# Two attentions over 257 keys on one Trainium2 core: scores in two halves, the last key in one product, heads summed on VectorE

## The reference, cut to what matters

```python
# x: (128, 32, 128), ctx: (128, 257, 128); 16 heads of 8 features
q = heads(x @ Wq.T); k = heads(ctx @ Wk.T); v = heads(ctx @ Wv.T)   # layer 1: q, k normalised per head
s = einsum('bhqd,bhkd->bhqk', q, k)                # layer 2: masked keys get -inf
p = softmax(s)                                     # over 257 keys
out = einsum('bhqk,bhkd->bhqd', p, v)
x = x + (join_heads(out) @ Wo.T + bo)
```

## Time and profile before

| | before |
|---|---|
| median of 3 runs | 4020.48 us (4013.39 to 4028.0) |
| profiled execution, first to last instruction | 4018.7 us |
| l1x_att, first to last scores | 827.0 to 1330.5 us |
| l2x_att, first to last scores | 1905.4 to 2469.8 us |
| PE, DVE, ACT, POOL busy in the whole | 78%, 60%, 51%, 49% |

### The profile page before, as it was taken

One profiled execution on the slowest core, in us unless ns is written; L12 is line 12 of the kernel. 1 busy time (PEld: TensorE's weight loads), 2 busy tenths in 40 slices (PEclk: granted clock), 3 DMA queues, 4 the chain that ended last, 5 costly groups with the idle time before them and its releaser, 6 DMA issues. The chain is left out here.

```text
span 4018.7 us, 81101 instructions
## 1 busy us (share of the span) xinstructions
PE 3136.4 (78%) x24323; PEld 2160.5 (54%) x24323; DVE 2425.2 (60%) x5893; ACT 2065.1 (51%) x6409; POOL 1963.5 (49%) x1960
## 2 busy tenths in 40 slices
PE   6969587779999597675999997788773458867966
PEld 4759434456666486553777775233332235744645
DVE  7956586656666474243666665698894312456862
ACT  5545306657777454323666665454541114557954
POOL 4630205656666695053555554788880251116830
PEclk9979698989999798787999998899896676987978
DMA  3300002312222000111111110443332125910000
GB/s 96 91 19 0 6 3 72 98 59 68 66 66 68 21 2 6 53 39 47 31 29 30 30 29 27 142 138 137 137 121 86 20 49 152 230 25 5 2 7 21
DMA packets 138613, 233.70 MB, mean 58 GB/s; under 512 B 28428, under 2 KB 100398, under 8 KB 137623
## 3 DMA queue, kind: packets, MB, share of 16 engines
q1 hardware_dynamic: 130264, 221.60, 18.8%
q0 software_dynamic: 8128, 9.45, 1.3%
HBM read 200.43 MB, written 13.71 MB: 53 GB/s over the span
## 5 line engine op out<-in xcount | busy, mean ns | idle before, releaser
L2427 POOL TENSOR_TENSOR l2x_att_prob<-l2x_att_prob,l2x_att_rs 128x1024 f32<-128x1024 f32 x128 | 242.2, 1893 | 253.2 <-DVE l2x_att_rs L2671 253.2
L3200 PE MATMUL l2a_pY<-l2a_hc,ident 128*128 128x512 f32 x512 | 275.0, 677 | 90.3 <-POOL l2a_hc L3119 56.1
L2427 POOL TENSOR_TENSOR l1x_att_prob<-l1x_att_prob,l1x_att_rs 128x1024 f32<-128x1024 f32 x128 | 242.2, 1893 | 190.6 <-DVE l1x_att_rs L2671 190.6
L2626 ACT ACTIVATE l2x_att_prob<-l2x_att_pS,l2x_att_nmx 128x257 f32<-128x257 f32 x512 | 236.2, 474 | 169.4 <-DVE l2x_att_nmx L2666 169.4
L3089 POOL TENSOR_TENSOR l2a_dbu<-l2a_dx,l2a_BC 128x1024 f32<-128x1024 f32 x128 | 298.5, 2352 | 21.5 <-PE l2a_pY L3200 10.7
L2626 ACT ACTIVATE l1x_att_prob<-l1x_att_pS,l1x_att_nmx 128x257 f32<-128x257 f32 x512 | 236.2, 474 | 129.7 <-DVE l1x_att_nmx L2666 129.7
L3217 ACT ACTIVATE l2a_pA<-l2a_dl,l2a_A 128x512 f32<-128x512 f32 x256 | 174.4, 689 | 188.8 <-DVE l2a_pH L3323 113.0
L3200 PEld LDWEIGHTS l2a_pY<-l2a_hc,ident 128*128 128x128 f32 x512 | 103.7, 211 | 253.2 <-issue 120.0
L3323 DVE TENSOR_TENSOR_SCAN l2a_pH<-l2a_pA,l2a_dbu 128x512 f32<-128x512 f32 x192 | 224.8, 1216 | 23.6 <-POOL l2a_dbu L3089 12.2
L2666 DVE TENSOR_REDUCE l2x_att_nmx<-l2x_att_pS 128x2 f32<-128x514 f32 x256 | 165.5, 688 | 115.7 <-PE l2x_att_pS L2534 113.0
L2666 DVE TENSOR_REDUCE l1x_att_nmx<-l1x_att_pS 128x2 f32<-128x514 f32 x256 | 165.5, 689 | 92.4 <-PE l1x_att_pS L2527 92.3
(11 more groups left out here) (735 smaller groups left out, 9284.2 us busy)
## 6 DMA issues: line engine op xcount, KB each, us to landing
l2a_BC<-l2a_rows SPq DMA_DIRECT2D x128, 512.0 KB, 3.8
l3x_att_ctn<-ctx_n SPq DMA_DIRECT2D x32, 576.0 KB, 13.9
l0x_att_kvs<-ctx_t SPq DMA_DIRECT2D x32, 514.0 KB, 3.5
l1x_k_xin<-ctx_t SPq DMA_DIRECT2D x32, 514.0 KB, 3.5
l1x_att_ctx<-ctx_t SPq DMA_DIRECT2D x128, 128.5 KB, 2.1
l1x_att_kT<-l1x_KA SPq DMA_DIRECT2D x128, 128.5 KB, 2.2
l2x_att_ctx<-ctx_t SPq DMA_DIRECT2D x128, 128.5 KB, 2.1
l3x_att_ctx<-ctx_t SPq DMA_DIRECT2D x32, 514.0 KB, 11.6
```

Of the source, the lines that this page charges most:

```text
L2427: pool.tensor_tensor(p, p, bc(rs[:, b, :], 2, LAST), ALU.mult).then_inc(scaled, 1)
L2626: last = act.activation(prob[:, b, j, 0:KEYS], pS[:, j, 0:KEYS], ACT.Exp, bias=nmx[:, b, j:j + 1], accum_out=sums[:, b, j:j + 1])
L3200: last = pe.matmul(pY[c][:, :], env.ident[:, :], hc[:, u % 3, c, :], start=False, stop=n == NS - 1)
```

## The change

- `scores` takes a half, u, and is called twice in a slot: groups 0 and 1 at the slot's start, groups 2 and 3 behind `attend`. Each waits only for its own half of p_made and announces itself once. In l2x_att the mask products are split in the same way.
- DVE takes maxima(n+1, 0), then factors(n), own_head(n-2), then maxima(n+1, 1).
- The last key: vm, tail, pbd and mt are laid out on all 128 partitions (32 for each group, half of it zeros, cleared once). `last_keys` is one product of 128 x 128, `turn_tails` four small products of 32 x 32, `pbd` 128 x 128, and its share of `output` one product. They now stand in slots 0 (last_keys) and 1 (turn_tails, pbd).
- DVE sums own over the four groups (`sum_heads`, a reduction of 128 x 512 to 128 x 128, tile osum) in slot 1, and `output` is one product osum x wo and one pbd x mt.
- On POOL the bias of x is added behind `queries`, and two memsets stand ahead of the loop.

```diff
@@ on TensorE
-                def scores(n, c, k):
+                def turn_tails():
+                    for h in range(R):
+                        r = slice(32 * h, 32 * h + 32)
+                        last = pe.matmul(PT[r, :], tail[r, :], env.ident[r, r])
+                    last.then_inc(pt_made, 1)
+
+                def last_keys(k):
+                    pe.wait_ge(vm_made, made(k))
+                    after(pe, mo_kept, k - 1)
+                    pe.matmul(M, vm[:, :, :].rearrange("p h j -> p (h j)"), wo[:, :]).then_inc(mo_made, 1)
+
+                def scores(n, c, k, u):
                     b = (c + 1) % 2
-                    pe.wait_ge(q_made, made(n))
...
-                    after(pe, p_made, 2 * (n - 1) + 1)
-                    for j in range(R):
+                    after(pe, p_made, 2 * (n - 1) + u)
+                    for j in (2 * u, 2 * u + 1):
                         r = slice(32 * j, 32 * j + 32)
...
+                    last.then_inc(s_made, 1)
...
                 def output(g):
-                    pe.wait_ge(own_made, made(4 * g + 3))
-                    for h in range(R):
-                        pe.matmul(X, own[:, h].rearrange("p b q -> p (b q)"), wo[:, :], start=h == 0, stop=False)
-                    pe.wait_ge(mo_kept, made(2 * g + 1))
+                    pe.wait_ge(osum_made, made(g))
+                    pe.matmul(X, osum[:, :, :].rearrange("p b q -> p (b q)"), wo[:, :], start=True, stop=False)
+                    pe.wait_ge(mo_kept, made(g))
                     pe.wait_ge(pb_made, made(g))
-                    for h in range(R):
-                        last = pe.matmul(X, pbd[:, h].rearrange("p b q -> p (b q)"), mt[:, h, :], start=False,
-                                         stop=h == R - 1)
-                    last.then_inc(out_made, 1)
+                    pe.matmul(X, pbd[:, :, :].rearrange("p b q -> p (b q)"), mt[:, :], start=False, stop=True
+                              ).then_inc(out_made, 1)
 
                 def slot(n, c, k):
                     if inside(n + 1):
-                        scores(n + 1, c, k)
+                        scores(n + 1, c, k, 0)
+                    if c == 1 and inside(n - 5):
+                        pe.wait_ge(tail_kept, made(2 * (k - 1) + 1))
                     if inside(n - 2):
                         attend(n - 2, (c - 2) % 4, k if c >= 2 else k - 1)
+                    if c == 1 and inside(n - 5):
+                        turn_tails()
+                    if inside(n + 1):
+                        scores(n + 1, c, k, 1)
                     if inside(n + 2) and KA is None:
                         keys(n + 2, c, k)
...
@@ on VectorE
+                def sum_heads(k):
+                    dve.wait_ge(own_made, made(4 * k + 3))
+                    after(dve, out_made, k - 1)
+                    dve.tensor_reduce(osum[:, :, :].rearrange("p b q -> p (b q)"),
+                                      own[:, :, :, :].rearrange("p h b q -> p (b q) h"), AX.X, ALU.add
+                                      ).then_inc(osum_made, 1)
...
                 def slot(n, c, k):
-                    if inside(n):
-                        factors(n, c)
                     if c == 2 and inside(n - 6):
                         add(k - 1)
                     if inside(n + 1):
                         maxima(n + 1, (c + 1) % 4, 0)
-                        maxima(n + 1, (c + 1) % 4, 1)
+                    if inside(n):
+                        factors(n, c)
                     if inside(n - 2):
                         own_head(n - 2, (c - 2) % 4, k if c >= 2 else k - 1)
-                    if c == 0 and inside(n - 4):
-                        dve.wait_ge(pt_made, made(k - 1))
+                    if c == 1 and inside(n - 5):
+                        keep_tails(k - 1)
+                    if inside(n + 1):
+                        maxima(n + 1, (c + 1) % 4, 1)
+                    if c == 1 and inside(n - 5):
+                        sum_heads(k - 1)
                     if inside(n + 2) and KA is None:
                         keys(n + 2, c)
-                    if c == 0 and inside(n - 4):
-                        keep_tails(k - 1)
                     if inside(n - 1):
                         keep_turned(n - 1, (c - 1) % 4)
```

More of the change, by code:

```diff
@@ L2370, in cross_attention @@
         cl, vt = st.sb("cl", [P, B]), st.sb("vt", [P, B])
-        m16, batch16 = st.sb("m16", [P, R, R]), st.sb("batch16", [16, BT])
-        vm, tail = st.sb("vm", [P, R, 16]), st.sb("tail", [P, BT, R])
-        pbd, mt = st.sb("pbd", [16, R, BT, S]), st.sb("mt", [16, R, D])
+        m16, batch32 = st.sb("m16", [P, R, R]), st.sb("batch32", [P, BT])
+        vm, tail = st.sb("vm", [P, R, 32]), st.sb("tail", [P, 32])
+        pbd, mt = st.sb("pbd", [P, BT, S]), st.sb("mt", [P, D])
+        osum = st.sb("osum", [P, BT, S])
         nmx, sums, rs = (st.sb(n, [P, 4, R]) for n in ("nmx", "sums", "rs"))
@@ L2415, in _ @@
                 st.open(pool)
+                pool.memset(vm[:, :, :], 0.0).then_inc(cleared, 1)
+                pool.memset(tail[:, :], 0.0).then_inc(cleared, 1)
                 pool.wait_ge(loaded, 16 * len(loads))
                 pool.wait_ge(vt_kept, 1)
+                pool.wait_ge(cleared, 2)
                 def queries(n, b):
@@ L2451, in slot @@
                         queries(n + 2, c + 2)
+                    if c == 0 and inside(n):
+                        x = env.X[:, k, :]
+                        pool.tensor_tensor(x, x, bo[:, :], ALU.add).then_inc(biased, 1)
                     if c == 1 and inside(n):
@@ L2528, in scores @@
                                          start=True, stop=not masked)
-                        if not masked and j % 2:
-                            last.then_inc(s_made, 1)
                     if masked:
-                        for j in range(R):
+                        for j in (2 * u, 2 * u + 1):
                             r = slice(32 * j, 32 * j + 32)
@@ L2642, in slot @@
                         values(n + 2, c)
-                    if c == 3 and inside(n):
-                        last_keys(k, 0)
                     if c == 0 and inside(n - 4):
-                        last_keys(k - 1, 1)
+                        last_keys(k - 1)
                 run_slots4(act, slot, B, -2, 3)
@@ L2691, in own_head @@
                     dve.wait_ge(o_made, made(n))
-                    after(dve, out_made, k - 1)
+                    if b == 3:
+                        dve.wait_ge(pt_made, made(k))
+                    if b == 0:
+                        after(dve, osum_made, k - 1)
                     o, m = O.rearrange("p (h q) -> p h q", q=S), bc(env.m4[:, :], 2, S)
```

70 lines of the change are left out of this document (27 added, 43 removed).

## The result

The changed kernel takes 4074.97 us (median of 4 runs, 4064.68 to 4082.06); the kernel before, beside it, 4020.24 us (4013.39 to 4028.0). The ratio is 1.0131, with a 95% interval of 1.0108 to 1.0154: 1.3% slower. Forecast were 4041.5 us. The direction is right and the time is inside the range, but of a loss of 21 us that was forecast, 55 came.

A forecast was written before the change was run, and what follows sets the result against it. TensorE was taken as busiest, with a ring over ACT's copy binding l1x_att and TensorE's work l2x_att, plus a kT wait in slot 1. +6 and +15 us made +21 on 4020.48: 4041.5 us, range 3997 to 4078.

The forecast's parts named there:

- A half costs as much as the whole: Scores on TensorE: each half another 0.65 us a slot in l1x_att, 0.76 in l2x_att; +2.6 and +3.0 us a round.
- The ring over ACT: l1x_att slots 2, 3, 0: attend, second-half scores, maxima, exponentials, ACT's probT copy, next attend; 3.88 us against TensorE's 3.4.
- The last key: TensorE: output from 16 passes to 4, 1.32 us less a round; turn_tails 0.2; the 0.80 wait for pbd goes.
- The first (PE alone): Rival: TensorE alone sets both stages, the new ring does not bind, kT in time; 3997 us, chance 0.12.
- The second and third (a half costs less): Rivals on scores: two groups cost half of four, 3918 us, chance 0.05; a half is 0.55, 4000 us, chance 0.05.
- The fourth: Rival on TensorE: new changes of shape cost 0.1 more at each half, together +39; 4080 us, chance 0.12.
- the forecast of +6: l1x_att: round 16.01 against 15.83, +0.18, times 32 rounds.

The follow-up runs named there:

- the two kernels that open the ring at different places: Changed kernel with factors ahead of the first maxima on DVE, 4031.91 us; changed kernel with queries ahead of scale on POOL, 4033.77 us.
- the kernel with factors first: Changed kernel with factors(n) ahead of maxima(n+1, 0) on DVE, as before the change: 4031.91 us, ratio 1.0004.
- With both opened: Changed kernel with queries ahead of scale on POOL and ACT's copy of probT between the two halves of the exponentials: 3983.97 us, ratio 0.9917.
- the best version: Changed kernel with score halves side by side, queries ahead of scale and keys ahead of sum_heads: 3873.37 us, ratio 0.9658.
- the sum behind the keys: Changed kernel with whole scores, factors ahead of the maxima and sum_heads behind the keys on DVE: 3943.31 us, ratio 0.9777.
- copy between: Changed kernel with factors ahead of the maxima and ACT's copy of probT between the two halves of the exponentials: 4032.81 us, ratio 1.0008.
- no sum: Changed kernel with whole scores, factors ahead of the maxima, and four output products in place of sum_heads: 3938.10 us, ratio 0.9787.
- halves adjacent: Changed kernel with both score halves side by side ahead of attend, a wait each, and queries ahead of scale: 3910.86 us, ratio 0.9698.
- queries first: Changed kernel with queries(n+2) ahead of scale(n) and tails on POOL: 4033.77 us, ratio 1.0012.

## Why the prediction was right and wrong

**The step that failed** is the sentence "POOL and ACT are far from full, and the memsets lie beside the loads: nothing for them." It prices POOL by how busy it is. The sum did work out a new ring, but only for ACT; it moved factors behind the first maxima, as the order on VectorE shows, and never asked who waits for factors. POOL's scale does, the queries stand behind scale, and PE's next scores wait for the queries. Every link was in the code. In the trace of before, scores and their weight loads waited for ACT's prob (44.0 us in the whole of l1x_att) and not for qb, because scale needed only exponentials that were already under way. The cost is 1.14 us a round in l1x_att and 0.50 in l2x_att, 50 to 52 us in both stages, shown by the two kernels that open the ring at different places.

**The rest of the sum was too dear, by 16 to 19 us.** With the ring open the stages stand 2.3 and 4.5 us above before, where the forecast had +21; so the two errors partly hid each other. Term by term, from the kernel with factors first unless said otherwise:

- *A half costs as much as the whole*: 0.65 forecast in l1x_att, 0.63 measured; 0.76 with the mask, 0.74 measured. Rows of four passes took 0.70, as the prediction said they would. Scores kept PE busy 115.69 us in 350 (2.96 us a round before, 5.60 after, 1.9 times; 2.0 forecast). Right.
- *The ring over ACT*: it exists and binds l1x_att once the ring over POOL is open, at 3.66, 3.76 and 3.78 in slots 2, 3 and 0, and not 3.88. In the changed kernel it is hidden, so attend didn't wait for probT there, as the prediction wanted to see. The sign of it was right, its size 0.10 to 0.22 too long in three slots.
- *The last key*: the four small products took 0.19 (0.2 taken); the pbd wait of 0.80 is gone; output is two products of 0.3 us in place of eight. Rows of the kernel after, slot 1 of l1x_att on PE:

```profile
1110.81 0.26 PE L2514 MATMUL l1x_att_pO<-ident,l1x_att_tail 32*32 32x32 f32 x8
...
1113.48 0.49 PE L2568 MATMUL l1x_att_pO<-l1x_att_wo,l1x_att_osum 128*128 128x128 f32 x2 [0.31 <-DVE l1x_att_osum L2685]
1113.81 0.39 PE L2571 MATMUL l1x_att_pO<-l1x_att_mt,l1x_att_pbd 128*128 128x128 f32 x2
```

- *sum_heads* was mis-sized: 1.06 us and not the 0.68 of the reduction in the earlier trace rows, which adds 32 numbers that lie side by side where this one adds four that lie 128 numbers apart. In l1x_att the output then waits 0.31, and slot 1 is 4.61 where 4.37 was forecast.
- *l2x_att*: PE's slot is 4.01, not 4.14, since from values to scores it is 0.54 and not the 0.64 that I carried over from l1x_att; slot 0 is 4.36, not 4.55. Slot 1 is 5.58, not 5.42: sum_heads starts 2.23 us after attend (2.24 forecast), but takes 0.39 longer than I had it; values start at 3.75 and not 3.37, and from output to the next attend 0.22 comes back (1.29 for 1.51). The wait is there as forecast, and only there (after, PE, slot 1 of l2x_att):

```profile
2119.32 0.64 PE L2562 MATMUL l2x_att_pO<-l2x_att_probT,l2x_att_v 128*32 128x128 f32 x16
...
2123.07 0.71 PE L2508 MATMUL l2x_att_pKV<-l2x_att_wv,l2x_att_ctx 128*128 128x128 f32 x4 [0.66 <-DVE l2x_att_kT L2673]
```

**The rivals.** The first (PE alone) fell: two rings bind, not none. With both opened, l1x_att does go to 14.79, near its 15.04, but the changed kernel has neither open. The second and third (a half costs less) fell by the 0.63. The fourth, 4080 us for costlier changes of shape, was nearest to the measured time and for the wrong reason: every hand-over from one shape to another cost what the earlier trace rows show or less. By the total alone it would have passed for the cause.

**Why one missed term was enough.** In l1x_att the forecast of +6 came from terms that nearly cancel: +2.6 us a round for scores, -1.3 for the output, and stalls that go. With such a sum a single missed term of 1 us a round is the whole answer.

## What to carry to other kernels

When an instruction is moved in an engine's order, follow its result, not only its own engine: who waits for it, what stands behind that waiter, and whether the chain comes back to what the moved instruction now stands behind. An engine that is half idle can still close a ring; its busy share says nothing on that. Splitting a product that uses the array's row groups side by side cost a full pass here for each part that stood alone (0.63 us for a half, 0.64 for the whole); if an early start is wanted, put the parts next to each other with a wait each, and look in how many slots they really run together.

## What the hardware showed that was not expected

- **Row groups issued under separate waits can still run side by side.** Two halves of 32x257 products, the second with its own wait, took 0.73 us together when both were ready, 1.26 when attend stood between. There the wait costs 0.09, not the overlap. Where the second half was late they took 1.28 to 1.42, as in two of four slots of l1x_att.
- **A reduction's time isn't its count of elements alone.** Reducing 128x512 to 128x128 took 1.06 us, to 128x16 0.68. Whether the stride of 512 bytes between the numbers that are added, or the eight times longer output, makes the difference was not tried.
- **The unchanged part of the program moves by more than some edits are worth.** Outside the two stages the same instructions took 2909.1 us in the profile of before, 2904.7 in after, 2884.1 in the best version and about 2937 with the sum behind the keys. Most of it lies in one sublayer, whose tiles are called l1f: from its first to its last instruction it took 172.2 us in before and 173.7 in after, 184.4 to 195.1 in the eight kernels from factors first to copy between, which ran on one chip, and 172.4 and 166.8 in the last two, on another. A second, l0f, took 123.9 us in three profiles (no sum, copy between, best) and 136 in the others; between halves adjacent and best the two sublayers make 36 of the 38 us. The granted clock doesn't tell these apart: between the stages it was 0.83 both in before and in queries first, where that part took 552.1 and 572.4 us. In steady stretches of the two stages it was 0.99 or 1.00 in every profile. So for edits of 15 us the length of the stages tells two kernels apart, and whole times don't, across chips least of all. Whether the chip itself sets the length of l1f was not tested; what sets it stays open.
